# Layer 0: ScalarE converts the first of a tile's four adjacency chunks instead of the last

## What is computed

```python
def layer0(h, adj):                       # h = relu(layernorm(x))
    e = (h @ Ws) @ (h @ Wt).T             # 8192 x 8192 scores
    alpha = softmax(where(adj > 0, e, NEG), axis=-1)
    return alpha @ (h @ Wc)
def layer1(h, adj):
    Wh = h @ W
    e = leaky_relu((Wh @ a1)[:, None] + (Wh @ a2)[None, :], 0.2)
    attention = softmax(where(adj > 0, e, NEG), axis=1)
    return elu(attention @ Wh)
x = x + layer0(relu(layernorm(x)), adj)
x = x + layer1(relu(layernorm(x)), adj)
```

## Time and profile before

| | us |
|---|---|
| median of 3 runs | 1520.61 |
| lowest and highest of them | 1518.73, 1529.33 |
| the profiled execution | 1534.86 |
| its span, first to last instruction | 1533.0 |
| busy in the span: TensorE, VectorE, ScalarE | 1311.9, 1272.6, 1043.3 |
| conversions of layer 0 on VectorE, first and last start | 98.2, 957.0 |

### The profile page before, as it was taken

How to read it: one execution, slowest core, us unless ns; L and a number is a source line. 1 busy time by engine, 2 the same in 40 slices (tenths; PEclk the granted TensorE clock), 3 DMA queues, 4 the chain that set the end, 5 groups by cost and what they waited for, 6 DMA issues and landing times.

```text
span 1533.0 us, 78545 instructions
## 1 busy us (share of the span) xinstructions
PE 1311.9 (86%) x31947; PEld 1143.1 (75%) x31947; DVE 1272.6 (83%) x2313; ACT 1043.3 (68%) x2064; POOL 1.5 (0%) x11
## 2 busy tenths in 40 slices
PE   1836879999999999999999898867899988988986
PEld 1625767887878888888888787754788878877986
DVE  5777779999989999999999898436798978977977
ACT  1835556667666777767666676467788877877975
POOL 0000000000000000000000000000000000000000
PEclk9977899999999999999999999989899999999999
DMA  7039879999999999999999998410333323323322
GB/s 228 0 154 341 284 267 367 360 370 369 363 363 359 386 365 375 370 377 369 378 364 363 356 346 306 128 31 0 92 100 113 113 72 100 112 72 100 113 72 79
DMA packets 114304, 363.21 MB, mean 237 GB/s; under 512 B 11504, under 2 KB 44528, under 8 KB 81392
## 3 DMA queue, kind: packets, MB, share of 16 engines
q1 hardware_dynamic: 114160, 361.02, 66.4%
HBM read 319.03 MB, written 41.94 MB: 235 GB/s over the span
## 4 chain that ended last, share of the span: by engine, by line
PE 47%; DMA 18%; issue 13%; DVE 12%; ACT 6%; DVEq 1%; SPq 1%; ACTq 1%
DMA arena<-in_adjB 17%; PE ps L809 15%; PE ps L796 9%; PE ps L708 5%; DVE arena L1347 4%; PE ps L729 3%; PE ps L670 3%; PE ps L702 3%; DVE arena L1322 3%; PE ps L703 2%; PE ps L658 2%; DVE mx L1356 2%; ACT arena L1002 2%; ACT arena L905 1%; PE ps L590 1%
## 5 line engine op out<-in xcount | busy, mean ns | idle before, releaser
L1495 DVE TENSOR_SCALAR arena<-arena 128x128 f32 (+1 forms) x768 | 202.6, 340 | 63.2 <-ACT arena L1052 58.2
L729 PE MATMUL ps<-arena 128*128 128x129 f32 x2048 | 248.0, 279 | 4.6 <-issue 4.6
L809 PE MATMUL ps<-arena 128*128 128x129 f32 x2048 | 247.6, 280 | 2.2 <-issue 2.2
L729 PEld LDWEIGHTS ps<-arena 128*128 128x128 f32 x2048 | 239.6, 195 | 4.9 <-issue 4.9
L809 PEld LDWEIGHTS ps<-arena 128*128 128x128 f32 x2048 | 239.5, 195 | 2.5 <-issue 2.5
L1322 DVE TENSOR_SCALAR arena<-arena 128x2048 fp8e4<-128x2048 int32 x192 | 234.8, 1224 | 7.6 <-DMA arena<-in_adjB 1.5
L988 ACT ACTIVATE arena<-ps 128x512 f32<-128x512 f32 x256 | 153.0, 598 | 124.8 <-PE ps L670 124.8
L982 ACT ACTIVATE arena<-ps 128x512 f16<-128x512 f32 x256 | 153.9, 601 | 62.6 <-PE ps L658 62.4
L796 PE MATMUL ps<-arena 128*32 128x132 f16 x8192 | 160.7, 231 | 41.4 <-issue 29.8
L1011 ACT ACTIVATE arena<-arena 128x2048 fp8e4<-128x2048 int32 x64 | 122.3, 1911 | 103.6 <-DMA arena<-in_adjB 103.6
L1052 ACT ACTIVATE arena<-ps 128x396 f32<-128x396 f32 (+1 forms) x384 | 151.1, 463 | 59.2 <-PE ps L796 59.2
(11 more groups left out here) (166 smaller groups left out, 1469.0 us busy)
## 6 DMA issues: line engine op xcount, KB each, us to landing
arena<-in_adjB SPq DMA_DIRECT2D x256, 1024.0 KB, 7.3
sel_pick<-arena SPq DMA_DIRECT2D x64, 256.0 KB, 9.6
sel<-arena SPq DMA_DIRECT2D x64, 256.0 KB, 9.6
arena<-sel_pick SPq DMA_DIRECT2D x64, 256.0 KB, 3.4
arena<-sel SPq DMA_DIRECT2D x64, 256.0 KB, 2.7
x_t<-in_x SPq DMA_DIRECT2D x64, 64.0 KB, 8.2
x_mid<-y_t SPq DMA_DIRECT2D x64, 64.0 KB, 8.5
arena<-x_mid SPq DMA_DIRECT2D x8, 512.0 KB, 4.9
```

Of the source, the lines that this page charges most:

```text
L729: last = nc.tensor.matmul(pv_ps, p_T[:, s * P:(s + 1) * P], v_sel[:, b, s, :], start=False, stop=(s == SB - 1), skip_group_check=True)
L809: last = nc.tensor.matmul(xv_ps[b], w_msk[:, b, s, :], x1_sel[:, b, s, 0:VW], start=False, stop=(s == SB - 1), skip_group_check=True)
L1495: last = nc.vector.tensor_scalar(w_raw[b][:, k, :], own, x1_sel[:, b, k, D + 2:D + 3], x1_sel[:, b, k, D + 1:D + 2], ALU.mult, ALU.max)
```

## The change

ScalarE's conversion takes chunk c0 in place of c3, at the same place in its order. VectorE's three conversions, at the same three places in its order, take c1, c2 and c3 in place of c0, c1 and c2. SyncE still issues c0, c1, c2, c3 in that order, but the first now waits for ScalarE's conversion and the other three for VectorE's.

```diff
             def load_chunk(t, c):
-                if c < 3:
-                    wait(sp, conv_done, t * 3 + (c - 2))
+                if c:
+                    wait(sp, conv_done, t * 3 + (c - 3))
                 else:
                     wait(sp, conv_act, t)
...
-                nc.tensor.matmul(dst, off_i[q // 3], m_sel8[:, b, 4 * q:4 * q + 4, :].rearrange("p s n -> p (s n)"),
+                nc.tensor.matmul(dst, off_i[q == 0], m_sel8[:, b, 4 * q:4 * q + 4, :].rearrange("p s n -> p (s n)"),
...
             def convert(t, b):
-                act.wait_ge(adj_in[3], t * 16 + 16)
-                wait(act, mg_done, t * 2 - 2)
+                act.wait_ge(adj_in[0], t * 16 + 16)
+                wait(act, mg_done, t * 2 - 3)
                 act.sem_inc(conv_settled, 1)
-                nc.scalar.activation(mask_8[:, b, 3 * QCH:4 * QCH, :], adj_st[:, 3, :, :], ACT.Sign, ...
+                nc.scalar.activation(mask_8[:, b, 0:QCH, :], adj_st[:, 0, :, :], ACT.Sign, ...
...
-                nc.vector.memset(bare[:, 0:3 * QCH], NO_EDGES)
-                nc.vector.memset(bare[:, 3 * QCH:NB], NO_EDGES_ACT)
+                nc.vector.memset(bare[:, QCH:NB], NO_EDGES)
+                nc.vector.memset(bare[:, 0:QCH], NO_EDGES_ACT)
...
                 if there(i, 0):
-                    convert(i, b, 0)
+                    convert(i, b, 1)
                 if there(i, 3):
                     maximum(c)
                 if there(i, 0):
-                    convert(i, b, 1)
+                    convert(i, b, 2)
                 if there(i, 1):
                     make_pick(e, 1 - b)
                 if there(i, 0):
-                    convert(i, b, 2)
+                    convert(i, b, 3)
```

More of the change, by code:

```diff
@@ L1006, in convert @@
             def convert(t, b):
-                act.wait_ge(adj_in[3], t * 16 + 16)
-                wait(act, mg_done, t * 2 - 2)
+                act.wait_ge(adj_in[0], t * 16 + 16)
+                wait(act, mg_done, t * 2 - 3)
                 act.sem_inc(conv_settled, 1)
-                nc.scalar.activation(mask_8[:, b, 3 * QCH:4 * QCH, :], adj_st[:, 3, :, :], ACT.Sign, bias=-0.5, saturate=False
+                nc.scalar.activation(mask_8[:, b, 0:QCH, :], adj_st[:, 0, :, :], ACT.Sign, bias=-0.5, saturate=False
                                      ).then_inc(conv_act, 1)
```

## The result

The changed kernel takes 1538.65 us (median of 9 runs, 1533.43 to 1552.71) against 1520.61 us (9 runs): 18 us or 1.1% slower, ratio 1.0113 with a 95% interval of 1.0076 to 1.015. The forecast was 1529, slower by 8. In the ratios of this document one run is left out as a slow one, the slowest of last_first (1565.2 us).

What follows compares the result with a forecast made beforehand. DMA transfers were the first suspect, with VectorE's floor 0.64 us a tile below the present 13.1. The new round's +11 us and -3 us for small terms made +8 on 1520.6: 1529 us, range 1501 to 1560.

Steps and rivals of the forecast that it cites:

- The new round: VectorE's second conversion to next mark 10.84, c0's issue 3.6, c2's landing 12.4: 26.8 us for two tiles, +11 us.
- The waits at L1011, L702 and L1356: ScalarE's for a chunk, TensorE's for exponentials, VectorE's for scores: should go, up to 0.4 us a tile for VectorE.
- VectorE's wait for chunks: At L1322, replacing the old waits: about 0.7 to 1 us a tile, most at the second conversion.
- so c2 becomes the late one: At VectorE's second conversion: c2 lands 2.7 us after the mark (VectorE's first conversion), wanted at 1.62.
- the faster rival: VectorE becomes the bound; c2 landing 1 us sooner gives 12.9 us a tile, about -15 us, 1505; chance 0.18.
- only just in time: At VectorE's third conversion: c3 there about 5.2 us after the mark, wanted at 5.07 plus what c2 has cost.
- the base of 13.2: Round of the kernel before, through c3, ScalarE, TensorE and VectorE: 26.4 us for two tiles, 13.2 each.
- The -3 us for the mask reduction: VectorE's mask reduction waited 6.4 us in all for ScalarE's conversion; half of that counted as gained.
- bandwidth alone: Transfers at 372 GB/s set 13.1 us a tile whatever the release order: 0 to -3 us, 1518 to 1521; chance 0.15.
- the floor of 12.46 us: VectorE's period with all three chunks in time: gain 34 us, 1487; needs 392 GB/s; chance 0.05.
- the +69 us: Issuing c0 2.6 us later in a two-tile round, 1.3 us a tile, if nothing covered it.
- The dry queue: At the end of a tile's transfers, c0 issued after c3 landed: +0.8 us a tile, +42 us, 1563; chance 0.17.

Runs made afterwards that it cites:

- last_first: The kernel before with SyncE loading the chunks in the order c3, c0, c1, c2, ScalarE still converting c3: 1555.8 us, ratio to before 1.0283.
- first_last: The changed kernel with load order c1, c2, c3, c0, so ScalarE's chunk is loaded last: 1526.06 us, ratio to before 1.0052.
- one_early: The changed kernel with load order c1, c0, c2, c3, one of VectorE's loads ahead of ScalarE's: 1488.71 us, ratio to before 0.9829.
- held_before: The kernel before with SyncE's load of c0 held until VectorE's second conversion instead of its first: 1559.79 us, ratio to before 1.0252.
- scalar_c2: The kernel before in load order c0, c1, c2, c3, with ScalarE converting c2 and VectorE c0, c1, c3: 1490.42 us, ratio to before 0.9796.
- scalar_third: The changed kernel with load order c1, c2, c0, c3, two of VectorE's loads ahead of ScalarE's: 1486.33 us, ratio to before 0.9804.
- third_two_stores: scalar_third with the store of the picked mask issued a second time into rows nobody reads: 1504.03 us, ratio to before 0.9886.
- after_two_stores: The changed kernel with the store of the picked mask issued a second time into rows nobody reads: 1550.89 us, ratio to before 1.0203.

## Why the prediction was right, and where it was not

*The direction, the range and the main term were right.* The new round was put at 13.4 us a tile; it measures 13.4, though in part by luck, as the next paragraph says. The release of c0 was taken at 3.6 us after the mark and came at 3.7. The waits at L1011, L702 and L1356 vanished as written, and VectorE's wait for chunks, forecast at 20 to 30 us in 400, is 20.8. That the release at SyncE's queue is the cause and not something beside it is shown from three sides: the order alone makes it (last_first), takes it away but for 0.5% (first_last), and a first load that goes out 2.3 us sooner moves the time by -3%, one that goes out 1.6 us later by +2.5% (one_early, held_before).

*The step that failed is "so c2 becomes the late one".* c2 landed 11.4 us after the first issue, not 12.4: the sooner landing that the faster rival had counted on did come, since c2 is now issued 1.3 us behind c0 instead of 5.1. But c3 did not follow: it was issued at 7.4 instead of 6.5 and landed after 15.3 us, just beyond my 14.6 to 15.2. VectorE waits on average 0.35 us for c2 and 0.41 for c3, not mostly for c2, and the chain runs through c3. I had c3 as "only just in time" and summed only c2. That the sum still came out is luck: with the measured 11.4 in place of 12.4 it gives 10.84 + 3.7 + 11.4 = 25.9 us for two tiles, 13.0 each, which is the small gain of the faster rival; the lateness of c3, which the sum left out, brought it back to 13.4.

*The sum was too small by 10 us.* The round did grow by about the 0.2 us that was forecast, against the profiled execution of before: 13.21 to 13.37 us over the last 53 steps, 9 us. But that execution lies 14 us above the median on which the +8 was then put, while the profiled execution of the changed kernel lies only 3 us above its own. That difference of 11 us and the 7 us between the two profiled executions are the 18. The step that was mis-sized is therefore the base of 13.2. The kernel before with a second store, profiled at 1519 us, took 13.05 over the same steps. The -3 us for the mask reduction were a guess that nothing here tests.

*The rival "bandwidth alone" fell*, by the runs with a second store and by one_early's 387 GB/s. With it fell my argument against the floor of 12.46 us, that 392 GB/s had never been held: scalar_c2 holds 389 GB/s and 12.5 us a tile. The page "DMA: Bandwidth & Descriptors" of the Trainium skill, which under its specifications gives the HBM limit of about 358 GB/s per core that the prediction cites, says below its table of measurements that this is a core's share when both cores of the HBM domain are streaming, while its single-core figures go up to 425 GB/s. The 405 GB/s measured here for 400 us with one core running agree with that; the 13.6 us a tile used the figure outside its case.

*The rule to issue early and wait late*, from the rules for kernel authors on the same page of the Trainium skill, was borne out in sign, though the +69 us that the prediction worked out with it was far too much here. The changed kernel at the same time took ScalarE and TensorE out of the round; that this makes up the difference is argued and not measured by itself. held_before has the late issue without that relief: +39 us for 1.6 us.

*The dry queue* did not come in the form that was priced: in every step of tiles 30 to 59 c0 was issued before c3 of the tile ahead had landed, 1.2 to 2.6 us before. What remains of it is small: the share fell from 1.00 to 0.98, 0.3 us a tile. A window of the changed kernel at the place that was named, the four to five us after the mark of 607.27:

```profile
611.50:612.50 1.00, 1.00 (x11) 1.00 (x10) 1.00 (x2) 1.00 (x2) 0.00 (x0) 1.00 0.99 192
```

The share is nearly full there and the rate is half: engines count as busy on packets that take long. Like the 372 GB/s at a share of 1.00, it says that the busy share does not show how much a queue could still carry.

*What stays open* is why the last chunk of a tile lands 3.1 to 4.2 us behind the third in every kernel with a late first issue, and 2.8 to 3.1 where the first goes out at 1.4 or 1.5, while the others mostly follow each other at 2.5 to 3.1. The packets show where the time goes. In the changed kernel the 8 KB packets that start between the landings of c2 and c3 take 0.50 us on average, and those between c0 and c1 0.31; in before and scalar_third the former take 0.34. About half of the bytes that move between c2 and c3 belong to the stores behind them, in all of these kernels. It is neither the memory of c3 (last_first) nor the number of bytes (third_two_stores has more, and 2.8). That it depends on what stands in the queue behind the last chunk fits most runs (after_two_stores, with one store more behind c3, has 3.2 against 3.9) but was not tried by itself.

## What to carry to other kernels

Where several engines free the buffers of one queue of loads, do not let a load whose buffer comes free late stand ahead of all that are free early. Loading in the order in which the buffers come free does this: here VectorE's first at 1.2 us after the mark, its second at 2.9, ScalarE's at 3.6, VectorE's third at 6.3. Put last, the slow consumer stretches the round through its own wait; put first, it stands at the head of the queue and holds loads whose buffers have long been free; third, it is 2% faster than last and 3% faster than first. Second (one_early) it is as fast as third, so the runs do not show that the exact order matters; what the fast kernels share is an early load ahead of ScalarE's and VectorE's third at the end. And a DMA share of 1.00 is no proof of a limit: add bytes that nobody needs and see whether the time moves.

## What was not expected of the hardware

The same 16 engines at a busy share of 0.97 to 1.02 moved 355 GB/s (held_before's mean from 450 to 850 us), 372 (before), 387 (scalar_third) and 405 GB/s (third_two_stores), over transfers of the same shapes; the first three carry the same loads and stores a tile and differ in when they are issued. The mean duration of an 8 KB packet in that stretch was 0.350 us before, 0.354 in the changed kernel, 0.339 in scalar_third and 0.324 in third_two_stores, while the usual packet takes 0.309: the difference is a share of 5 to 15% of packets that take over 0.4 us.
